# Conditional FFN with expert LoRA: first-step loads and splits reordered, and four pairs of rank matmuls moved one tile ahead

## The reference

```python
hidden_i  = einsum('bsd,fd->bsf', x, wi)
hidden_i += ALPHA * (x @ common_wi_a.T) @ common_wi_b.T
hidden_i += expert_lora(x, ids, experts_wi_a, experts_wi_b)      # also times ALPHA
hidden_i  = relu(hidden_i)
hidden_o  = einsum('bsf,df->bsd', hidden_i, wo)
hidden_o += ALPHA * (hidden_i @ common_wo_a.T) @ common_wo_b.T
hidden_o += expert_lora(hidden_i, ids, experts_wo_a, experts_wo_b)
return x + hidden_o
```

## Time and profile before

| | us |
|---|---|
| median of 3 runs | 120.17 |
| lowest, highest | 119.84, 120.77 |
| the profiled execution | 120.01 |
| its span, first to last instruction | 118.2 |

### The profile page before, as it was taken

The page is one execution under the profiler, slowest core; times in us unless marked ns, Lnnn a source line. Parts: engine busy times, 40 slices in busy tenths (PEclk is TensorE's granted clock), DMA queues, the critical chain, the costliest instruction groups (busy, mean ns, idle before and its releaser), DMA issues.

```text
span 118.2 us, 1984 instructions
## 1 busy us (share of the span) xinstructions
PE 113.1 (96%) x730; PEld 103.7 (88%) x730; DVE 60.3 (51%) x104; ACT 47.4 (40%) x94; POOL 42.0 (36%) x60
## 2 busy tenths in 40 slices
PE   6979998989999999999999999999999999999990
PEld 6758887878889999988889999988889999999990
DVE  4486999999964421134444335134444135525121
ACT  4467589343973511323663523213343113332100
POOL 2024699989899020225573006616000020000000
DMA  3999799998980035106000015006000010111121
GB/s 97 372 358 361 222 367 370 333 310 287 246 309 7 6 64 205 44 3 222 0 6 0 0 48 176 30 20 188 33 0 0 0 38 11 44 44 44 44 94 44
DMA packets 8748, 14.93 MB, mean 126 GB/s; under 512 B 1042, under 2 KB 5138, under 8 KB 8738
## 3 DMA queue, kind: packets, MB, share of 16 engines
q1 hardware_dynamic: 8018, 13.49, 34.9%
q10 hardware_dynamic: 720, 1.31, 3.2%
HBM read 12.70 MB, written 2.10 MB: 125 GB/s over the span
## 4 chain that ended last, share of the span: by engine, by line
PE 77%; DVE 11%; DMA 5%; SPq 3%; issue 1%; ACT 1%
PE bank_o L732 36%; PE bank_h L627 24%; PE bank_o L728 5%; DMA b_raw<-in_rec_b 5%; PE bank_h L661 5%; DVE hid L475 4%; DVE common_st L475 2%; PE bank_low L678 2%; PE bank_o L751 1%; DVE xT L480 1%; DVE low_stack L475 1%; PE bank_o L627 1%; PE bank_low L627 1%; DVE b_stack L491 1%; PE bank_h L704 1%
## 5 line engine op out<-in xcount | busy, mean ns | idle before, releaser
L732 PE MATMUL bank_o<-wcat,hid 128*128 128x272 f32 x336 | 45.1, 289 | 0.0
L732 PEld LDWEIGHTS bank_o<-wcat,hid 128*128 128x128 f32 x336 | 43.4, 188 | 0.0
L627 PE MATMUL bank_h<-xT,wiT 128*128 128x512 f32 x156 | 39.8, 395 | 0.6 <-DVE wiT L562 0.6
L627 PEld LDWEIGHTS bank_h<-xT,wiT 128*128 128x128 f32 x156 | 27.7, 189 | 6.4 <-issue 1.2
L475 DVE SCALAR_TENSOR_TENSOR hid<-bank_h,hid 128x512 fp32r<-128x512 f32 x26 | 17.3, 687 | 13.4 <-ACT hid L379 13.4
L379 ACT ACTIVATE hid<-bank_h 128x512 fp32r<-128x512 f32 x26 | 14.9, 598 | 17.1 <-PE bank_h L661 16.9
L552 DVE TENSOR_TENSOR o_sb<-bank_o,x_nat 128x256 f32<-128x256 f32 x16 | 6.7, 423 | 19.5 <-PE bank_o L751 17.4
L276 POOL TENSOR_TENSOR b_stack<-b_raw,b_stack 32x1024 fp32r<-32x1024 f32 x6 | 14.4, 2406 | 3.5 <-ACT b_stack L367 3.4
L267 POOL CAST a_stack<-a_raw 128x192 fp32r<-128x192 f32 x8 | 4.5, 560 | 18.1 <-DMA a_raw<-in_rec_a 18.1
L661 PEld LDWEIGHTS bank_h<-low_stack,b_stack 128*128 128x128 f32 x52 | 8.7, 189 | 2.0 <-DVE low_stack L475 0.6
L402 ACT ACTIVATE rank_sb<-bank_o 128x64 fp32r<-128x64 f32 x14 | 3.1, 223 | 18.0 <-PE bank_o L732 18.0
(11 more groups left out here) (58 smaller groups left out, 107.5 us busy)
## 6 DMA issues: line engine op xcount, KB each, us to landing
b_raw<-in_rec_b SPq DMA_DIRECT2D x8, 512.0 KB, 5.6
x_nat<-in_x_n SPq DMA_DIRECT2D x4, 512.0 KB, 3.9
out<-o_sb SPq DMA_DIRECT2D x16, 128.0 KB, 1.7
x_raw<-in_x_t SPq DMA_DIRECT2D x6, 256.0 KB, 4.0
w_raw<-in_wo_t SPq DMA_DIRECT2D x4, 256.0 KB, 5.2
w_raw<-in_wi_t ACTq DMA_DIRECT2D x3, 256.0 KB, 4.9
a_raw<-in_rec_a SPq DMA_DIRECT2D x8, 96.0 KB, 3.8
bo_raw<-in_rec_bo SPq DMA_DIRECT2D x8, 96.0 KB, 3.6
```

Of the source, the lines that this page charges most:

```text
L627: nc.tensor.matmul(up_bank(q, m)[:, :], wiT_at(sw, k, m), xT[q % 2][sx][:, k, :], start=start, stop=False)
L732: last = nc.tensor.matmul(bank_o[g % NO][:, 0:WIN], hid[q % 2][sh][:, m, tok], wcat[sw][:, m, win], start=(m == 0 and i == 0), stop=(m == ...
```

## The change

- Loads: wi piece 0 becomes a tensor of its own, wi_0, in which each half is contiguous. On ACT's queue only wi piece 1 stays. Pieces 2 and 3 go to SP's queue behind b of step 0, and common moves ahead of x and a of step 1.
- ACT: b_stack goes ahead of wi piece 2, ranks_in_hi(0) ahead of wi piece 3.
- DVE: the same for the low parts, and common_b ahead of the low parts of x of step 1.
- POOL: split_common goes ahead of split_a(1).
- PE: up_lora 0 to 3 of step 0 stand behind tile 4, ahead of tile 5.

```diff
             sp.dma_start(idt[:, :], ids.rearrange("(o n) -> o n", o=1)).then_inc(ids_in, 16)
             for k in range(KD):
-                sp.dma_start(w_raw[:, 0, k * 2 * P:(k + 1) * 2 * P], wi_t[0][:, k * 2 * P:(k + 1) * 2 * P]).then_inc(wi0_in[k], 16)
+                sp.dma_start(w_raw[:, 0, k * 2 * P:(k + 1) * 2 * P], wi_0[k]).then_inc(wi0_in[k], 16)
...
             load_b(0)
+            for i in range(2, PIECES):
+                sp.dma_start(w_raw[:, i, :], wi_t[i - 1]).then_inc(wi_in[i], 16)
+            sp.wait_ge(common_zero, 1)
+            for i in range(3):
+                sp.dma_start(common_raw[i * BLK:i * BLK + R, :], common).then_inc(common_in, 16)
             load_x(1)
             for n in range(PAIR):
                 expert.append(sp.value_load(idt[0:1, PAIR + n:PAIR + n + 1], min_val=0, max_val=E - 1))
                 load_a(1, n)
-            sp.wait_ge(common_zero, 1)
-            for i in range(3):
-                sp.dma_start(common_raw[i * BLK:i * BLK + R, :], common).then_inc(common_in, 16)
             load_b(1)
...
             split_a(0)
             pool.wait_ge(a_ready, PAIR)
+            split_common()
+            pool.wait_ge(common_a_lo, 1)
             split_a(1)
             pool.wait_ge(a_ready, 2 * PAIR)
-            split_common()
-            pool.wait_ge(common_a_lo, 1)
...
-            for i in range(1, PIECES):
-                act.dma_start(w_raw[:, i, :], wi_t[i]).then_inc(wi_in[i], 16)
+            act.dma_start(w_raw[:, 1, :], wi_t[0]).then_inc(wi_in[1], 16)
...
-                for i in range(1, PIECES):
-                    split_wi_hi(i)
+                split_wi_hi(1)
                 split_b_hi(0, 0)
                 split_b_hi(0, 1)
+                split_wi_hi(2)
                 ranks_in_hi(0)
+                split_wi_hi(3)
...
-                for i in range(1, PIECES):
-                    split_wi_lo(i)
+                split_wi_lo(1)
                 split_b_lo(0, 0)
                 split_b_lo(0, 1)
+                split_wi_lo(2)
                 ranks_in_lo(0)
+                split_wi_lo(3)
+                common_b()
                 for k in range(KD):
                     split_x_lo(1, k)
-                common_b()
...
                 up_main(0, 4)
-                up_main(0, 5)
                 for m in range(4):
                     up_lora(0, m)
+                up_main(0, 5)
                 up_main(0, 6)
                 up_main(0, 7)
...
+    wi_0, wi_t = wi_t[0].reshape(P, KD, 2 * P).transpose(1, 0, 2), wi_t[1:]
```

More of the change, by code:

```diff
@@ L15, with conditional_ffn @@
 STAGES = [("up", 0), ("up", 1), ("down", 0), ("up", 2), ("down", 1), ("up", 3), ("down", 2), ("down", 3)]
-def conditional_ffn(nc, x_t, x_n, ids, wi_t, wo_t, rec_a, rec_b, rec_bo, rec_ao, common, out):
+def conditional_ffn(nc, x_t, x_n, ids, wi_0, wi_t, wo_t, rec_a, rec_b, rec_bo, rec_ao, common, out):
     P = 128
@@ L22, in conditional_ffn @@
     D = KD * P
-    PIECES = wi_t.shape[0]
+    PIECES = wo_t.shape[0]
     PIECE = wi_t.shape[2]
@@ L861 @@
     common = np.concatenate([given["common_wo_a"], given["common_wo_b"].T], axis=1)
-    laid = dict(x_t=x_t, x_n=x_n, ids=ids, wi_t=wi_t, wo_t=wo_t, rec_a=rec_a, rec_b=rec_b, rec_bo=rec_bo, rec_ao=rec_ao, common=common)
+    laid = dict(x_t=x_t, x_n=x_n, ids=ids, wi_0=wi_0, wi_t=wi_t, wo_t=wo_t, rec_a=rec_a, rec_b=rec_b, rec_bo=rec_bo, rec_ao=rec_ao, common=common)
     nc = bacc.Bacc("TRN2", target_bir_lowering=False, num_devices=1)
```

## The result

The changed kernel takes 120.98 us in the median of 14 runs, beside 119.95 for the kernel before in 14 runs: 1.008 of before, 95% interval 1.0054 to 1.0106. It is slower by about 1 us. The profiled execution took 121.09 us for a span of 119.3. Medians are of all executions; ratios and intervals leave out those that came out over 1.5% above the fastest of their kernel, most of them at a lower granted clock.

What follows compares the result with a forecast made beforehand. The prediction took the line from b through DVE to up_lora(1, 0) as the bound. b's 1.29 us gain was given back by two weight splits (1.24), giving -0.1: 119.9 us, 8-in-10 range 118.9 to 121.2.

Steps and rivals of the forecast that it cites:

- What bounds the kernel: The line from the second b through DVE sets PE's up_lora(1, 0) at 24.60 us; PE then runs without a break.
- PE's work is the limit: Rival: low_stack comes right behind its input, up_lora(1, 0) at 23.75, 0.85 us earlier; 118.8 to 119.4 us, chance 0.24.
- the landing of b: Loads: with wi pieces 2 and 3 behind it, the second b lands 1.29 us earlier, at 9.47.
- the sum: DVE's line: 11.80 + 5.86 + 1.24 = 18.90 us for the first hidden_lo, 0.05 earlier than before.
- the tail behind that mark: Loads: b lands 0.97 us behind the point where all bytes up to its end have moved.
- the landing of common: Loads: 3.06 MB through near 10.4 us, common landing 0.97 behind, about 11.4.
- The stretch on DVE: From b_stack's end to the first hidden_lo: 5.86 us as before, plus 1.24 for two weight splits.
- PE's order: up_lora 0 to 3 ahead of tile 5: nothing added; 0.9 us lost waiting for low_stack, paid from slack.
- Wi piece 0's wait: PE's 0.6 us wait for the second half could go or stay; taken as 0, deciding nothing while b is later.
- b isn't earlier: Rival: b stays at 10.76 and the two weight splits add 1.24 us; about 121.2 us, chance 0.11.
- POOL first: Rival: POOL's 2.39 us subtraction precedes the second weight split, up_lora(1, 0) 2.3 us later; to 122.3 us, chance 0.12.

Runs made afterwards that it cites:

- pe_only: The kernel before with only the rank matmuls up_lora 0 to 3 moved ahead of tile 5; 120.51 us beside 120.41, 1.005 of before.
- common_back: The changed kernel with common back in its old places in the loads, on POOL and on DVE; 120.74 us, 1.011 of before.
- after_act_cast: The changed kernel with common's 96x1024 cast on ACT behind x of step 1 instead of on POOL; 1.008 of before.
- gate: The changed kernel with wi pieces 2 and 3, common and all later loads on SP's queue issued only after the second b landed; 1.019 of before.
- common_order_only: The kernel before with only common's new order on POOL and DVE, its load unmoved; four runs took 121.05 to 123.67 us beside 119.99.
- pe_back: The changed kernel with the rank matmuls of tiles 0 to 3 back behind tile 5; 121.03 us, 1.015 of before.
- wi23_act: The changed kernel with wi pieces 2 and 3 back on ACT's queue; 124.26 us, 1.034 of before.
- wi0_strided: The changed kernel with wi piece 0 loaded from the strided layout of before; two runs took 122.97 and 120.92 us.
- weights_only: The kernel before with only the new order of the weight splits on ACT and DVE; 122.87 us, 1.021 of before.
- no_common_lo: The changed kernel without POOL's subtraction on common, leaving out the low part of its first factor; 119.85 us, 1.003 of before.
- before_act_cast: The kernel before with common's 96x1024 cast on ACT behind x of step 1 instead of on POOL; 119.30 us, 0.993 of before.

## Why the prediction was wrong

The forecast was 0.1 us faster; the profiled execution came out 1.08 us slower.

- *What bounds the kernel* was right: the line of b through DVE sets up_lora(1, 0) before and after, and PE runs without a break behind it. What was missing is the second line. POOL's, at 23.55, stood only 1 us behind; in pe_only, common_back, after_act_cast, gate and common_order_only it ended last. The rival "PE's work is the limit" reckoned without it.
- *The first step that failed is the landing of b*, on DVE's line: "b lands 1.29 us earlier, at 9.47". It landed 0.41 earlier, and the 0.88 between are most of the 1.2 us by which the sum is off. Half of the 0.88 is the flow: the step lets 2.29 MB pass "at the same total rate", by 8.5, and it took until 8.9. The dip to 221 and 168 GB/s, where before had 394 and 359, is some 0.18 MB, about the missing 0.4 us; by all profiles it goes with pieces 2 and 3 leaving ACT's queue. Which of a's short packets and the late start of b fills that time so poorly wasn't settled. The other half is the tail behind that mark, taken as fixed at 0.97 us: it was 1.4, and 0.5 in gate with nothing queued behind b (2.29 MB through by 9.0, b at 9.50). That the transfers behind b lengthen it is likely and not shown (one profile each).
- *The second is the landing of common*, "landing 0.97 behind, about 11.4". It landed at 14.0: 3.06 MB were through at 11.6 and not at 10.4, and common came 2.4 us behind that mark. Why is open. This sets POOL's line, which the sum doesn't have. With split_common first on POOL, this alone would have made the kernel slower: where POOL's line ends last, PE follows 0.14 to 0.15 us behind (the table), so with DVE's line on time up_lora(1, 0) would have come at about 25.2, an estimate from 25.03 + 0.15, still 0.6 later than before. So b's landing alone is at most about half of the loss. In gate, with b at 9.50 and common at 15.09, POOL's line did end last.
- *The stretch on DVE*, 5.86 + 1.24 = 7.10, came out at 7.38. The sum was nearly right by luck, as its make-up was not: with common at 14.0 the second weight split ran free, and the third stood behind POOL's cast (1.45 instead of 0.62).
- *PE's order* was right in that it costs nothing: pe_back and pe_only show no price. That up_lora(0, 0) came at 14.17 (forecast 14.25) is luck: the forecast has low_stack held up by POOL's cast, and it was held up by the later b. Wi piece 0's wait moved and decided nothing, as taken.
- *The rivals.* "b isn't earlier", at 121.2 with a chance of 0.11, is nearest to what happened, though b did come 0.41 earlier and POOL's line has no part in it. POOL first did not occur: in no run did POOL's subtraction stand ahead of the second weight split.

Open is why b landed at 12.1 to 12.4 in wi23_act, wi0_strided and weights_only, and at 9.7 to 11.0 in kernels with nearly the same loads.

## What to carry to other kernels

Follow every line that meets at the wait that sets the end, not only the one that ended last: here a second one stood 1 us behind, and edits that freed the first bought nothing. A transfer moved from ahead of the critical one to just behind it may still be in its way: bytes ahead divided by the rate gave 9.5 us, and 10.0 to 10.4 came in most runs. Where two engines can't do their work at the same time, look for a third one: ACT's cast gave 0.993 on the kernel before, where a new order gave a loss. It gave nothing on the changed kernel, where ACT's own input was late.

## What the runs showed of the hardware

- DVE and POOL stood in each other's way: common_b's first instruction, 96x256, took 2.49 us beside POOL's subtraction (2.42 of them in the chain), 1.13 behind POOL's cast (no_common_lo) and 0.28 with POOL idle (before_act_cast).
- The landing of a 512 KB load may depend on what is queued behind it: 9.50 us with nothing, 10.31 with two 256 KB loads, one profile each, where runs with the same loads differ by up to 0.7 us and a few land at 12 or later.
- Three 80 KB loads to 16 partitions each, issued at 6.5 to 7.6 us behind other loads, landed no earlier than when they were issued at 10.3 to 11.2 (14.0 in both).
- After PE had waited 2.1 us and then 1.0 us (wi23_act), the granted clock stood at 0.56 and 0.58 in the stretches from 16 to 20 us, near the lower of its two levels (1.2 of 2.4 GHz): twelve matmuls of tiles 5 and 6 took 3.15 us instead of 2.75. After a wait of 2.4 us in weights_only it was 0.50 and 0.64 there. A wait of 0.7 us left it at 1.00 in the changed kernel. So here a late load cost more than its wait.
